# A decoder layer on one core: denominators by ln and exp, first loads rearranged, two steps moved to GpSimd, a new order of all steps

## The reference

```python
# part a: causal linear attention, 16 heads of 16
q, k, v = split(layernorm(x) @ w_attn.T)
phi = lambda t: elu(t) + 1
num, den = causal sums over s <= t of (phi(q_t) . phi(k_s)) v_s and of phi(q_t) . phi(k_s)
x = x + (num / (den + 1e-6)) @ w_proj.T
# part b: attention over ctx by a divergence of probabilities, then an MLP of 1024
q_prob, k_prob = prob(layernorm(x)), prob(ctx)            # tanh, sum, clip
sid = einsum(q_prob - k_prob, log(q_prob) - log(k_prob))
f = (ctx - softmax(-sid / 16) @ ctx) @ W_diff.T + b_diff + layernorm(x)
x = x + layernorm(gelu(layernorm(f) @ W1.T + b1) @ W2.T + b2 + f)
# part c: on n = layernorm(x): the 128 tokens with the highest n @ w_router
h = rmsnorm(n[idx]);  causal softmax attention, 16 heads;  gated feed-forward of 682
out = x + n with the chosen rows of n replaced
```

## Time and profile before

| | us |
|---|---|
| median of three runs | 887.78 |
| profiled execution, span | 886.5 |
| TensorE busy | 810.7 (91%) |
| VectorE busy | 724.2 (82%) |
| ScalarE busy | 560.2 (63%) |
| GpSimd busy | 276.6 (31%) |

### The profile page before, as it was taken

One profiled execution on the slowest core, in us unless ns is written; L12 is line 12 of the kernel. 1 busy time (PEld: TensorE's weight loads), 2 busy tenths in 40 slices (PEclk: granted clock), 3 DMA queues, 4 the chain that ended last, 5 costly groups with the idle time before them and its releaser, 6 DMA issues.

```text
span 886.5 us, 21236 instructions
## 1 busy us (share of the span) xinstructions
PE 810.7 (91%) x7219; PEld 699.5 (79%) x7219; DVE 724.2 (82%) x1689; ACT 560.2 (63%) x1518; POOL 276.6 (31%) x443
## 2 busy tenths in 40 slices
PE   7778799999999999999999999999999999988875
PEld 4567678888888888888898888888898888867644
DVE  4777789898988989898998989898998989784642
ACT  3463548577676758577666758577667758575541
POOL 0021514234251524234251514333251514233211
PEclk8899999999999999999999999999999999999999
DMA  8310111202020110102020111202020111101010
GB/s 295 101 42 25 48 50 37 61 19 84 18 83 6 47 53 36 59 18 83 18 83 6 55 45 36 65 12 83 18 83 6 59 41 36 55 2 49 8 54 7
DMA packets 31223, 44.02 MB, mean 50 GB/s; under 512 B 2512, under 2 KB 23120, under 8 KB 31184
## 3 DMA queue, kind: packets, MB, share of 16 engines
q1 hardware_dynamic: 27696, 32.93, 10.9%
q0 software_dynamic: 2048, 6.30, 2.4%
q10 hardware_dynamic: 1440, 4.28, 1.5%
HBM read 28.81 MB, written 14.70 MB: 49 GB/s over the span
## 4 chain that ended last, share of the span: by engine, by line
PE 56%; DVE 16%; ACT 15%; issue 8%; DMA 2%; POOL 2%; SPq 1%; DVEq 0%; ACTq 0%; POOLq 0%
PE bank L1131 14%; ACT w_raw_or_stage_c L721 9%; PE bank L1235 4%; PE bank L1253 4%; PE bank L1315 3%; PE bank L1509 3%; PE bank L1390 3%; PE bank L1323 3%; PE bank L1139 3%; PE bank L1293 3%; PE bank L1147 3%; ACT L721 2%; PE bank L1415 2%; DVE prob L915 2%; PE bank L1435 2%
## 5 line engine op out<-in xcount | busy, mean ns | idle before, releaser
L676 ACT ACTIVATE prob<-bank,b_folded 128x256 f32<-128x256 f32 x128 | 53.7, 471 | 99.9 <-PE bank L1131 99.7
L870 DVE TENSOR_TENSOR a_s<-bank,const 128x512 f32<-128x512 f32 x112 | 72.6, 685 | 47.5 <-PE bank L1235 25.8
L721 ACT ACTIVATE w_raw_or_stage_c<-bank,c_nmax 128x128 f32<-128x128 f32 x256 | 90.2, 403 | 3.2 <-DVE c_nmax L1044 3.0
L538 POOL DMA_INDIRECT out<-w_raw_or_stage_c,row_of_slot_out x16 | 17.3, 1081 | 182.1 <-DVE w_raw_or_stage_c L1098 182.1
L721 ACT ACTIVATION_READ_ACCUMULATOR w_raw_or_stage_c<-bank,c_nmax 128x1 f32 x256 | 62.0, 242 | 0.0
L787 DVE TENSOR_TENSOR b_s_lo<-prob,b_s_hi 128x512 fp32r<-128x512 f32 x64 | 43.2, 675 | 21.0 <-ACT b_s_hi L563 21.0
L1426 PE MATMUL bank<-const,w_raw_or_stage_c 128*128 128x128 f32 x256 | 40.3, 280 | 16.6 <-ACT w_raw_or_stage_c L721 16.6
L860 DVE RECIPROCAL a_e<-a_e 128x512 f32<-128x512 f32 x16 | 53.5, 3342 | 0.0
L1426 PEld LDWEIGHTS bank<-const,w_raw_or_stage_c 128*128 128x128 f32 x256 | 28.0, 140 | 26.1 <-ACT w_raw_or_stage_c L721 16.9
L1131 PE MATMUL bank<-b_s_hi,w_mlp_hi 128*128 128x256 f32 x256 | 45.1, 298 | 2.5 <-ACT prob L676 1.4
L1044 DVE TENSOR_REDUCE c_nmax<-bank 128x4 f32<-128x512 f32 x64 | 41.7, 677 | 6.4 <-PE bank L1415 6.4
(11 more groups left out here) (256 smaller groups left out, 2698.7 us busy)
## 6 DMA issues: line engine op xcount, KB each, us to landing
token_rows<-norm_x_rms SPq DMA_DIRECT2D x16, 513.0 KB, 3.9
x_in<-in_x SPq DMA_DIRECT2D x16, 256.0 KB, 3.4
x<-in_x SPq DMA_DIRECT2D x16, 256.0 KB, 2.8
qc<-in_ctx SPq DMA_DIRECT2D x16, 256.0 KB, 2.7
b_f<-in_ctx_t SPq DMA_DIRECT2D x16, 256.0 KB, 2.9
out<-w_raw_or_stage_c SPq DMA_DIRECT2D x16, 256.0 KB, 2.2
w_raw_or_stage_c<-in_w ACTq DMA_DIRECT2D x4, 512.0 KB, 5.8
w_raw_or_stage_c<-in_w_gu ACTq DMA_DIRECT2D x4, 341.0 KB, 3.1
```

Source lines behind the costliest of these rows:

```text
L676: act_in(prob[:, 2 * (j % 2) + n, :], b0[:, n * T:(n + 1) * T], ACT.Gelu, bias=b1p[:, f:f + 1]).then_inc(b_gelu.sem, 1)
L721: act_in(c_e[g % 2][:, j * R:(j + 1) * R], C_SCORES[g][:, j * R:(j + 1) * R], ACT.Exp, bias=c_nmax[:, n:n + 1], accum_out=c_den[:, head:he ...
L870: tt(heads(A_MASKED[t][n][:, :]), heads(A_SCORES[n][:, :]), tri.unsqueeze(1).broadcast_to([P, 4, P]), ALU.mult).then_inc(a_scput.sem, 1)
```

## The change

- **Inverse.** ScalarE computes e = exp(−ln(den + eps)) in two ACTIVATEs. VectorE does one Newton step with scalar_tensor_tensor: a_dnear reads the bank a0, (den + eps) e; a_dinv makes (near − 2) e; a_y multiplies with −1 as well. a_score_0 waits for a_dnear. The table set natural_log_exp_and_others is preloaded at the start; a_qout of the first row no longer loads it.
- **c_ob** becomes one add x2 + c_norm on GpSimd, c_obs goes; **c_keep** goes from VectorE to GpSimd; adds of eps on GpSimd take constants from memory.
- **First loads.** The factors of the weights (cols) and the constants come right behind the first three weights; ctx, x, w_diff and the rest only when the next x has been asked for and the three weights are split. One semaphore becomes three. The scaling of part c's weights moves from c_rstd to a_rstd.
- **Order.** ORDER, WEIGHTS_AT and WARM_AT are new throughout: 162 products of ones instead of 69, besides the 14 at the start. On TensorE a_den now stands directly behind b_fd; on GpSimd c_rms1 stands ahead of c_h2rms and c_ob ahead of c_pick; on VectorE b_pnorm stands ahead of c_h2put; five of the weight splits go to round 2.

```diff
-b_ghi_3+ c_exp_1+ c_max_3+ c_w9 c_etp_2+ c_exp_2+ a_tp c_exp_3+ c_etp_3+ b_v c_dtp+ c_rms1 b_glo_3+ c_etput_0+
...
+b_down_3+ c_etp_1+ c_exp_0+ b_glo_3+ c_etp_2+ a_tp c_max_3+ b_ghi_2+ b_normed b_v b_ghi_3+ b_qb c_rms1 c_etp_3+
...
-WEIGHTS_AT = {(0, "c_w0"): 2, (0, "a_qout"): 1, (0, "c_w1"): 1, (1, "c_w2"): 1, (1, "c_w3"): 1, (1, "c_w4"): 2, (1, "c_w5"): 1, (1, "c_w6"): 1, (1, "c_w7"): 1, (1, "c_w8"): 1, (1, "c_w9"): 1}
...
+WEIGHTS_AT = {(0, 'c_etput_2'): 2, (0, 'c_mean'): 1, (1, 'a_ktp'): 1, (1, 'c_y'): 2, (1, 'c_score'): 1, (1, 'c_etput_0'): 1, (2, 'a_kq'): 1, (2, 'a_score_1'): 1, (2, 'b_glo_1'): 1, (2, 'b_gelu_1'): 1, (2, 'a_normed'): 1}
...
             sp.dma_start(const[:, 0:EARLY], consts[:, 0:EARLY]).then_inc(const_in.sem, 16)
-
             for n in range(NRAW):
-                if n == DC:
-                    sp.dma_start(const[:, EARLY:NCONST], consts[:, EARLY:NCONST]).then_inc(const_rest.sem, 16)
                 sp.dma_start(raw[:, n, 0:loads[n][1]], loads[n][0]).then_inc(raw_in[n].sem, 16)
-            sp.dma_start(x1[:, :, :], x_rows[0]).then_inc(a_kept.sem, 16)
-            sp.dma_start(qc[:, TT:2 * TT, :], ctx_rows[0]).then_inc(ctx_in_s.sem, 16)
-            sp.dma_start(b_f1[:, :, :], ctx_t_rows[0]).then_inc(ctx_t_in.sem, 16)
-            sp.dma_start(bc[:, :, :], vec_bc).then_inc(vec_in.sem, 16)
-            sp.dma_start(cols[:, :], vec_cols).then_inc(vec_in.sem, 16)
-            sp.dma_start(wcqk[:, :, :], w_cqk).then_inc(vec_in.sem, 16)
-            sp.dma_start(wcv[:, :, :], w_cv).then_inc(w_plain.sem, 16)
-            sp.dma_start(wo[:, :, :], w_out).then_inc(w_plain.sem, 16)
-            sp.dma_start(wd[:, :, :], w_diff).then_inc(wd_in.sem, 16)
+            sp.dma_start(cols[:, :], vec_cols).then_inc(cols_in.sem, 16)
+            sp.dma_start(const[:, EARLY:NCONST], consts[:, EARLY:NCONST]).then_inc(const_rest.sem, 16)
...
             next_x(0)
+            sp.wait_ge(raw_hi.sem, NRAW)
+            sp.dma_start(qc[:, TT:2 * TT, :], ctx_rows[0]).then_inc(ctx_in_s.sem, 16)
+            sp.dma_start(b_f1[:, :, :], ctx_t_rows[0]).then_inc(ctx_t_in.sem, 16)
+            sp.dma_start(x1[:, :, :], x_rows[0]).then_inc(a_kept.sem, 16)
+            sp.dma_start(wd[:, :, :], w_diff).then_inc(wd_in.sem, 16)
+            sp.dma_start(bc[:, :, :], vec_bc).then_inc(rows_in.sem, 16)
+            sp.dma_start(wcqk[:, :, :], w_cqk).then_inc(w_qk_in.sem, 16)
+            sp.dma_start(wcv[:, :, :], w_cv).then_inc(w_plain.sem, 16)
+            sp.dma_start(wo[:, :, :], w_out).then_inc(w_plain.sem, 16)
...
+                power(b, a_mean, a_mv[:, :, 1], a_rs[:, :], a_rstd)
                 if first(b):
-                    pool.wait_ge(vec_in.sem, 48)
+                    pool.wait_ge(cols_in.sem, 16)
+                    pool.wait_ge(w_qk_in.sem, 16)
                     pool.wait_ge(w_plain.sem, 32)
                     for k in range(DC):
                         for w, factor in ((wcqk[:, k, 0:D], 1.0 / HD ** 0.5), (wcqk[:, k, D:2 * D], 1.0), (wcv[:, k, :], 1.0)):
                             nc.gpsimd.tensor_scalar(w, w, g1_col[:, k:k + 1], factor, ALU.mult, ALU.mult) \
                                 .then_inc(w_scaled.sem, 1)
...
+            def c_ob_(b):
+                pool.wait_ge(*c_normed(b))
+                if not first(b):
+                    pool.wait_ge(*out_done(b - 1))
+                nc.gpsimd.tensor_tensor(ob[:, :, :], x2[:, :, :], c_norm[:, :, :], ALU.add).then_inc(c_ob.sem, 1)
...
+            def c_keep_(b):
+                pool.wait_ge(*c_idxput(b))
+                if not first(b):
+                    pool.wait_ge(*y_stored(b - 1))
+                    pool.wait_ge(*c_next(b - 1))
...
+                nc.gpsimd.tensor_scalar(index_out[:, :], index[:, :], batch_at[:, 0:1], None, ALU.add).then_inc(c_kept.sem, 1)
+                pool.wait_ge(*c_kept(b))
...
+                nc.gpsimd.tensor_scalar(batch_at[:, :], batch_at[:, :], float(T), None, ALU.add).then_inc(c_next.sem, 1)
...
                     if loads[n][3:]:
-                        act_e.wait_ge(vec_in.sem, 48)
+                        act_e.wait_ge(cols_in.sem, 16)
...
             def a_qout_(b):
-                nc.scalar.preload_act_table_set("natural_log_exp_and_others")
+                if not first(b):
+                    nc.scalar.preload_act_table_set("natural_log_exp_and_others")
                 act_e.wait_ge(*a_qk(b, 1))
                 act_in(a_e0[:, :], a1[:, :], ACT.Exp).then_inc(a_qout.sem, 1)
                 act_in(flat(qT[:, :, :]), a1[:, :], ACT.Relu).then_inc(a_qout.sem, 1)
...
             def a_dput_(b):
                 act_e.wait_ge(*a_den(b))
-                act_in(a_e1[:, :], a0[:, :], ACT.Identity, bias=C["den_eps"]).then_inc(a_dput.sem, 1)
+                act_in(a_e1[:, :], a0[:, :], ACT.Ln, bias=C["den_eps"]).then_inc(a_dput.sem, 1)
+                act_e.wait_ge(*a_dput(b, 1))
+                act_in(a_e1[:, :], a_e1[:, :], ACT.Exp, scale=-1.0).then_inc(a_dput.sem, 1)
...
-            def c_ob_(b):
-                act_e.wait_ge(*c_obs(b))
-                if not first(b):
-                    act_e.wait_ge(*out_done(b - 1))
-                for t in range(TT):
-                    act_in(ob[:, t, :], x2[:, t, :], ACT.Identity, bias=c_offset[:, t:t + 1], scale=c_gain[:, t:t + 1]) \
-                        .then_inc(c_ob.sem, 1)
...
+            nc.scalar.preload_act_table_set("natural_log_exp_and_others")
...
+            def a_dnear_(b):
+                dve.wait_ge(*a_dput(b))
+                stt(a_near, a0[:, :], DEN_EPS, a_e1[:, :], ALU.add, ALU.mult).then_inc(a_dnear.sem, 1)
+
             def a_dinv_(b):
-                dve.wait_ge(*a_dput(b))
-                nc.vector.reciprocal(a_e1[:, :], a_e1[:, :]).then_inc(a_dinv.sem, 1)
+                dve.wait_ge(*a_dnear(b))
+                stt(a_e1[:, :], a_near, 2.0, a_e1[:, :], ALU.subtract, ALU.mult).then_inc(a_dinv.sem, 1)
...
-                tt(flat(a_norm[:, :, :]), a0[:, :], a_e1[:, :], ALU.mult).then_inc(a_y.sem, 1)
+                stt(flat(a_norm[:, :, :]), a0[:, :], -1.0, a_e1[:, :], ALU.mult, ALU.mult).then_inc(a_y.sem, 1)
...
-                    dve.wait_ge(*c_obs(b - 1))
...
+                    dve.wait_ge(*c_kept(b - 1))
...
                         pe.wait_ge(*a_mask(b))
-                        pe.wait_ge(*a_dput(b))
+                        pe.wait_ge(*a_dnear(b))
                         pe.wait_ge(*a_kput(b))
```

103 lines of the change are left out of this document (43 added, 60 removed).

## The result

The changed kernel takes 901.5 us (median of 4 runs, 900.66 to 902.59) against 887.9 for the kernel before on the same chip: a ratio of 1.0159, 95% interval 1.0145 to 1.0172. It is slower by 14 us, where 881 and faster were forecast. The profiled execution has a span of 898.8 us.

A forecast was written before the change was run, and what follows sets the result against it. The prediction took TensorE to bound the kernel. From the profiled 886.5 us it summed −12 (start), +7 (14 rounds) and −2 (end) to 879.5, and with 1.3 to the median forecast 881 us; range 862 to 896.

The forecast's parts named there:

- Score_0: Scores on TensorE: a new wait of 1.2 us a round for loads, Ln, Exp and dnear; bounds 0 and 2.4.
- The start: First rows: earlier table, factors and denominators, and less VectorE work, save 12 us together; bounds −8 and −15.
- The old waits: TensorE's waits in the steady round, mainly at etp and xo: 2.0 us taken as gone; bounds 0 and 2.0.
- c_dtp: TensorE's wait for the reciprocals' broadcast, behind the copy of b_v on ScalarE: 0.8 us a round; bounds 0 and 1.2.
- h2tp's term: TensorE's wait for c_h2put, behind b_pnorm's four operations (1.4 us) on VectorE: 0.4 us a round; bounds 0 and 1.4.
- c_ob's: GpSimd: c_ob's add of 1.3 us, ahead of c_pick, fits into the gather's 2.90 us wait for token rows.
- The round's sum: Steady round: +1.2 − 2.0 + 1.3 = +0.5 us, counted in 14 rounds as +7.
- The end: Last round: c_rms1 ahead of c_h2rms on GpSimd lets the gather come 2 us earlier: −2; bounds +1 and −5.
- C: Rival: VectorE as a queue, blocked at dnear, makes TensorE wait again at up_0; round +1.9, 900 us; chance 0.20.
- D: Rival: the start's gain doesn't reach the end, 8 of the 12 us given back; 889 us; chance 0.15.
- E: Rival: a table switch on ScalarE costs more than its load; round +3.1, 917 us; chance 0.03.
- B: Rival: old waits go and ScalarE's chain hides; round −0.8, 863 us; chance 0.17 together with loads not running.

The follow-up runs named there:

- after: The changed kernel itself, as the change describes it, against the kernel before; 901.5 us, ratio 1.0159.
- old_loads: The changed kernel with its first loads issued in the order of the kernel before, the bulk ahead of the weights' factors; 903.8 us, ratio 1.0186.
- old_start: old_loads with the fourth weight's split and its fold also back ahead of the first exp of q; 907.8 us, ratio 1.0232.
- qb_first: The changed kernel with c_rstd behind b_qb on GpSimd, nothing else moved; 890.7 us, ratio 1.0035.
- ob_slot: The changed kernel with c_ob behind b_fnormed on GpSimd and tanh's table loaded ahead of the wait for its input; 900.8 us, ratio 1.0160.
- one_load: The changed kernel with a table set holding both functions loaded ahead of Ln, one load instead of two; 890.5 us, ratio 1.0031.
- kept_late: one_load with b_kept's add on GpSimd waiting until VectorE's b_fnormed is done; 880.6 us, ratio 0.9923.
- best_x: best with SP asking for the next x at the head of its round; 856.4 us, ratio 0.9643.
- best: Joins one_load, kept_late, qb_first and ob_slot on the changed kernel, with c_dbc ahead of b_vput on ScalarE; 868.6 us, ratio 0.9792.

## Why the prediction was wrong, point by point

- **Score_0, the inverse's price:** right, the mechanism too. 1.2 was forecast, 1.38 came. Counted from the start of the sexp copy (454.89 in after), Exp ended at +6.8 and dnear at +7.5, where +6.7 and +7.5 were forecast. There were 13 loads at each of the two lines, not 14.
- **The start:** better than forecast. The −12 was meant for the first row's sum with x, where −14.0 came (48.99 to 34.98); at the first denominators it was 6.0 + 3.6 = 9.6, where 11.9 came; at the fourth row 8 to 10, where 14.8 came. It reached the end. The parts were wrong: for the factors that came late and the early table I had 6.0, but the loads' order gave 1.5 and the split's place 3.8 (old_loads, old_start). The other 6.6 (denominators directly behind their inputs, the table, warm-up) were not separated.
- **The old waits:** I took 2.0 as gone. They went, but were 0.60, 0.23 and 0.64 in the round, 1.5 together: rows 4 divide by all 16 rows, filling and draining among them.
- **c_dtp:** 0.8 forecast, 0.55 measured.
- **The step that failed** is the price of the moves around GpSimd in the new order: h2tp's term, with b_pnorm's four operations at 1.4 and a wait of 0.4, and c_ob's, "so the add fits in there". I priced what stands in GpSimd's queue, and not what its adds do to VectorE beside them. Beside b_qb's add the four took 2.36, and h2tp waited 0.90 in place of 0.4; beside c_ob's add c_sel took 1.33, and idx waited 0.67 in place of nothing. qb_first and ob_slot remove these waits one by one. "c_keep and the adds with constants cost nothing: GpSimd idles 33 of 50 us" argues in the same way, but no run tests those operations.
- **The round's sum:** +2.03 came, +0.5 was forecast. Of the 1.5 between, idx makes 0.67, h2tp 0.5, the old waits, taken too large, 0.5, score_0 0.2 and c_dtp −0.25. Without the two waits the round would be at +0.46. That this is the forecast is luck in part: the old waits gave 0.5 less than I took, while c_dtp cost 0.25 less and h2tp 0.4 less (nothing is left of its wait in qb_first), and the one hides the other.
- **The time's sum:** of the 20.5 us between 881 and 901.5 the rounds make 17 (24 for 7), the end 5, the start −3, and 1.4 is the distance of this profiled execution from the median.
- **The end:** −2 forecast, +3.1 measured. c_rms1 did gain, though less than the 2 forecast: in after the gather's wait on VectorE is 1.60 in place of 2.81 (timeline of VectorE, last round):

```profile
865.89 0.35 DVE L1033 TENSOR_SCALAR c_rden_or_products<-picked_rows 128x256 f32<-128x256 f32 x1 [1.60 <-DMA picked_rows<-token_rows,row_of_slot]
```

  But ScalarE stood 3.15 us in the round ahead of it with nothing to wait for that the trace shows:

```profile
813.03 0.58 ACT L746 ACTIVATE w_raw_or_stage_c<-bank,c_rms_half 128x384 f32<-128x384 f32 x1
816.75 1.09 ACT L565 ACTIVATE prob<-bank 128x512 f32<-128x512 f32 x2 [3.15 <-issue]
```

  In one_load, which differs by the table loads alone, that stall is not there, and from the last denominators to the end it takes 128.2 us, as the kernel before (128.1); so without it the end would not be 2 shorter either. All seven runs of the new order with two loads a row have a stall of 2.2 to 3.4 us at this place, and none of the five with one or none of them. The rounds at the end are written out, and packets of the instruction queue lie in that stretch, so late instructions are a likely cause; no run tested it, and it stays open.
- **The rivals:** C gave 900, close to the time, and the period of 51.70 is over the 50.7 that was to be its sign. But the mechanism was another: in after TensorE waited at score_0 alone for that part of VectorE's queue, not a second time at b_fnormed's transposes or at up_0; where b_fnormed did become late (one_load), it was the add beside it, and kept_late mended that with VectorE's order untouched. D and E fell (old_start; 1.30 from load to ACTIVATE). B's round, under before's, came only with the edits of best_x.

## What to carry to other kernels

An idle GpSimd is not free: ahead of moving an add to it, or along it, look up which VectorE operations will run beside it and where their operands lie. In these runs those fed from PSUM kept their time, and the ones that grew had all their operands in SBUF; not every one of those grew, and where VectorE began first the add grew instead. When such an add moves, name the next neighbour too, and the DMAs that wait for it and stand ahead of others in their queue. Two functions that follow each other on ScalarE may load two tables though one set holds both; read the loads in the order or the trace, and load the common set by hand.

## What the hardware showed that was not expected

- One GpSimd add over 128x512 (1.27 to 1.41 us) lengthened what ran beside it on VectorE: four tensor_scalars of 128x256 by 0.98 us (1.38 to 2.36), two by 0.96 (0.73 to 1.69), two of 128x128 in bf16 by 0.90 (0.43 to 1.33), a scalar_tensor_tensor of 128x512 with its operands in SBUF by 0.74 (0.68 to 1.42). The add itself was hardly longer there; where it began second, in qb_first, it took 1.57 and VectorE's operations kept their time.
- Behind a single wait of 2.36 us in a round that is otherwise full the granted clock fell in every second round (means of 0.82 and 0.84 in two slices of 5 us), at 1.6 us each time; behind waits of 1.38 (after) and 1.53 us (best) it stayed at 1.00.
- Ln and Exp directly behind each other, after a tanh, took a load each, 13 of each in the profile, until one load of a common set was put ahead; that was worth 11 us.
